# A Mamba-2 block with a quantised FFN on one core: high and low parts of the stationary tiles interleaved element by element, and shifted by 32, 64 and 96 bytes

## The reference, cut to what matters

```python
x = hidden_states                       # (2, 512, 512)
xn = layernorm(x)
# attention part (a Mamba-2 layer)
proj = xn @ in_proj_w.T                 # gate 8192, xBC 10240, dt 128 channels
gate, xBC, dt = split(proj)
xBC = silu(causal_conv4(xBC))           # per channel, 4 taps
xs, B, C = split(xBC)                   # 128 heads of 64; 8 groups of B and C, 128 wide
Y = ssd(xs, B, C, D, dt)                # chunks of 128 tokens
yg = Y * silu(gate)
out = yg * rsqrt(mean(yg**2 by group) + eps) * norm_w
s = out @ out_proj_w.T                  # 8192 -> 512
# FFN part, weights packed as 4-bit pairs with scales
h = silu(xn @ W1.T) * (xn @ W3.T)       # 512 -> 1376
g = silu(h @ W2.T)                      # 1376 -> 512
return x + s * g
```

## Time and profile before

| what | value |
|---|---|
| time, median of 3 runs | 1780.93 us (1780.87 to 1780.94) |
| the profiled execution | 1780.88 us, its span 1779.1 us |
| granted TensorE clock over the span | 0.999 of 2.4 GHz |
| TensorE matmul busy | 1764.8 us, 99% |
| VectorE, ScalarE, GpSimd busy | 80%, 69%, 71% |

### The profile page before, as it was taken

How to read it: one execution, slowest core, us unless ns; L and a number is a source line. 1 busy time by engine, 2 the same in 40 slices (tenths; PEclk the granted TensorE clock), 3 DMA queues, 4 the chain that set the end, 5 groups by cost and what they waited for, 6 DMA issues and landing times.

```text
span 1779.1 us, 30329 instructions
## 1 busy us (share of the span) xinstructions
PE 1764.8 (99%) x10357; PEld 1462.5 (82%) x10357; DVE 1427.7 (80%) x2196; ACT 1227.7 (69%) x2456; POOL 1261.9 (71%) x877
## 2 busy tenths in 40 slices
PE   8999999999999999999999999999999999999999
PEld 7788888888888888888888888888888888888877
DVE  7978878888788788788788887887887888878941
ACT  6986777777776777777867777677777677643320
POOL 5677787777777787677776787778776877676630
PEclk9999999999999999999999999999999999999999
DMA  5533343333333243333333333333333332235522
GB/s 197 165 124 101 100 131 108 94 122 107 117 107 111 97 134 96 101 111 119 117 105 98 117 124 96 116 101 115 122 90 112 109 127 96 78 109 166 150 77 95
DMA packets 122595, 202.84 MB, mean 114 GB/s; under 512 B 23056, under 2 KB 60560, under 8 KB 122192
## 3 DMA queue, kind: packets, MB, share of 16 engines
q1 hardware_dynamic: 120720, 197.32, 35.4%
q10 hardware_dynamic: 1728, 3.65, 0.5%
HBM read 193.57 MB, written 7.34 MB: 113 GB/s over the span
## 4 chain that ended last, share of the span: by engine, by line
PE 96%; DVE 2%; POOL 1%; issue 1%; DMA 0%; ACT 0%; SPq 0%; POOLq 0%; DVEq 0%
PE bank L135 17%; PE bank L137 17%; PE bank L136 16%; PE bank L544 11%; PE bank L586 7%; PE bank L632 6%; PE bank L634 6%; PE bank L633 6%; PE bank L832 3%; PE bank L694 3%; PE bank L675 1%; DVE z L1190 0%; PE bank L655 0%; DVE x_in L1342 0%; POOL yt L1523 0%
## 5 line engine op out<-in xcount | busy, mean ns | idle before, releaser
L1519 POOL TENSOR_TENSOR yt<-yt,ec 128x384 f32<-128x384 f32 x128 | 174.7, 1365 | 320.4 <-DVE ec L1254 320.4
L1190 DVE SCALAR_TENSOR_TENSOR z<-bank,cw_all,z 128x511 f32<-128x511 f32 (+2 forms) x477 | 356.2, 747 | 11.7 <-ACT z L945 0.4
L906 ACT ACTIVATE lm<-lm,hp 128x128 f32<-128x128 f32 x1024 | 313.2, 390 | 0.8
L135 PE MATMUL bank<-xn_hi,conv_hi 128*128 128x512 f32 x640 | 261.1, 408 | 3.5 <-DVE z L1190 3.5
L1224 DVE SCALAR_TENSOR_TENSOR lm<-lm,gm 128x1024 f32<-128x1024 f32 x128 | 261.0, 2039 | 3.5 <-ACT lm L906 3.5
L1245 DVE TENSOR_TENSOR xdt<-bank,hp 128x512 f32<-128x512 f32 x128 | 88.3, 690 | 212.8 <-PE bank L694 212.7
L137 PE MATMUL bank<-xn_hi,conv_lo 128*128 128x512 f32 x640 | 251.0, 392 | 0.0
L136 PE MATMUL bank<-xn_lo,conv_hi 128*128 128x512 f32 x640 | 250.7, 392 | 0.0
L1523 POOL TENSOR_TENSOR yt<-yt,gate 128x512 f32<-128x512 f32 x128 | 226.7, 1771 | 19.0 <-POOL yt L1519 0.9
L1528 POOL TENSOR_TENSOR conv_lo<-raw_x,conv_hi 128x512 fp32r<-128x512 f32 x124 | 218.9, 1766 | 9.8 <-ACT conv_hi L845 9.7
L135 PE MATMUL bank<-xn_hi,gate_hi 128*128 128x512 f32 x512 | 212.4, 415 | 0.0
(11 more groups left out here) (145 smaller groups left out, 3950.3 us busy)
## 6 DMA issues: line engine op xcount, KB each, us to landing
lm<-cs_d SPq DMA_DIRECT2D x128, 512.0 KB, 4.1
raw_x<-w_conv_dram SPq DMA_DIRECT2D x128, 256.0 KB, 3.1
ec<-e_d SPq DMA_DIRECT2D x256, 96.0 KB, 3.7
raw_o<-w_out_dram SPq DMA_DIRECT2D x64, 256.0 KB, 2.7
raw_g<-w_gate_dram SPq DMA_DIRECT2D x61, 256.0 KB, 2.8
raw_b<-w_conv_dram SPq DMA_DIRECT2D x32, 256.0 KB, 3.9
q_raw<-w1q_dram SPq DMA_DIRECT2D x10, 256.0 KB, 3.6
q_s<-w1s_dram SPq DMA_DIRECT2D x10, 256.0 KB, 3.9
```

Of the source, the lines that this page charges most:

```text
L135: pe.matmul(dst, a_hi, b_hi, start=(i == 0), stop=False)
L906: e = act.activation(lm[m % 3][:, u, :], lm[m % 3][:, u, :], ACT.Exp, bias=hp[bd.seq][:, Q_CS, k1, u:u + 1])
L1190: dve.scalar_tensor_tensor(dst[:, d:SEQ], src[:, 0:SEQ - d], cw_all[:, bd.group, pos, 3 - d:4 - d], dst[:, d:SEQ], ALU.mult, ALU.add).then ...
```

## The change

A new helper allocates a high and a low part together, as one tile whose last dimension is 2: element j of the high part is word 2j and that of the low part word 2j + 1. So a weight load still takes 128 words, each 8 bytes behind the one before, over 1024 bytes. ScalarE now writes each high part with a step of 8 bytes, and GpSimd reads it and writes the low part with that step. This holds for the stationary tiles of all five families. The moving tiles (`xn`, `wout`, `w2`) keep separate high and low parts.

Unnamed pads shift the tiles:

```diff
+        def alloc_pair(stack, name, shape):
+
+            t = alloc(stack, name, shape + [2], R32)
+            return t[:, :, :, 0], t[:, :, :, 1]
+
...
-        conv_hi = [alloc(main, f"conv_hi{i}", [KT, P], R32) for i in range(3)]
-        conv_lo = [alloc(main, f"conv_lo{i}", [KT, P], R32) for i in range(3)]
+        alloc(main, "off_c", [8])
+        conv_hi, conv_lo = zip(*[alloc_pair(main, f"conv_w{i}", [KT, P]) for i in range(3)])
...
-        gate_hi = [alloc(main, f"gate_hi{h}", [KT, HALF], R32) for h in range(2)]
-        gate_lo = [alloc(main, f"gate_lo{h}", [KT, HALF], R32) for h in range(2)]
+        alloc(main, "off_g", [8])
+        gate_hi, gate_lo = zip(*[alloc_pair(main, f"gate_w{h}", [KT, HALF]) for h in range(2)])
...
+        alloc(main, "off_o", [16])
         pre = ExitStack()
...
+        alloc(pre, "off_l", [24])
         wdt_lo = alloc(pre, "wdt_lo", [KT, P], R32)
+        alloc(pre, "past_y", [DIM])
...
-        y_hi = alloc(main, "y_hi", [2, SEQ], R32)
-        y_lo = alloc(main, "y_lo", [2, SEQ], R32)
+        alloc(main, "off_y", [24])
+        y_hi, y_lo = alloc_pair(main, "y_w", [2, SEQ])
...
-        up_hi = [[alloc(ctx, f"up_hi{i}{k}", [KT, P], R32) for k in range(2)] for i in range(2)]
-        up_lo = [[alloc(ctx, f"up_lo{i}{k}", [KT, P], R32) for k in range(2)] for i in range(2)]
+        up_hi, up_lo = zip(*[zip(*[alloc_pair(ctx, f"up_w{i}{k}", [KT, P]) for k in range(2)]) for i in range(2)])
...
-        h_hi = alloc(ctx, "h_hi", [MT + 1, SEQS * SEQ], R32)
-        h_lo = alloc(ctx, "h_lo", [MT + 1, SEQS * SEQ], R32)
+        h_hi, h_lo = alloc_pair(ctx, "h_w", [MT + 1, SEQS * SEQ])
```

## The result

The changed kernel takes **1803.36 us** (median of 4 runs, 1803.07 to 1804.4) against 1780.93: 22.4 us more, a ratio of 1.0127 with an interval of 1.0109 to 1.0144. The forecast of a modest gain has the wrong sign. The time lies in the range, among the slower cases. Lines in the changed file stand 6 further down from the allocations on.

What follows compares the result with a forecast made beforehand. TensorE's matmuls, busy 99% of the span, were taken to bound the kernel by their distances of starts. From 1780.9 us, less 8.3 for uneven and 5.8 for even stretches, 0 for the rest: 1766.8 us, range 1755 to 1806 (0.82).

Steps and rivals of the forecast that it cites:

- modest gain: Whole kernel: the likeliest case, 1755 to 1778 us around 1767, chance 0.45.
- the 96-column stretch: Four FFN groups with 96 weight columns: 230.0 ns a distance despite shorter loads, taken as best sign that TensorE's readers disturb each other.
- Fixed: TensorE's matmuls: changing weights costs what it costs; as the prediction's rival of no change, 1781 us, chance 0.18.
- The step of 8 bytes in the weight loads: Stationary tiles of all families: load and stream go at one pace, ending their disturbance; 8.3 us plus 5.8 us less.
- The 5.8 us for the even ones: 5751 evenly spaced matmuls in convolution, gate, output projection and FFN: each distance 1 ns shorter, 5.8 us less.
- The 8.3 us for the uneven stretches: 128 gate groups and 160 convolution groups: distances of 230.0 and 229.0 ns fall to 226.7, 8.3 us less.
- no change: Whole kernel: 13.3 ns is the cost of changing weights, unevenness comes from something else such as fp32 groups; 1781 us, chance 0.18.
- the left-over is the same at either width: TensorE's matmuls of 512 and 256 columns: 13.3 ns beyond streaming at both, ascribed to weight load or change of weights.
- The 1 ns from 388 against 389: One matmul without a load beside it took 388 ns, neighbours 389; the difference taken as gain for each even distance.
- The slower rival: Whole kernel: leaving equal steps and starts costs 3.3 ns a matmul, 1792 us, or twice 13.3 ns, 1849 us; chance 0.29.
- The fp32 matmuls: Plain fp32 matmuls between the families, operands now starting 32 bytes apart: 5 us either way, taken as 0.
- ScalarE and GpSimd: Their writes and reads with 8-byte steps: at most 1.5 us more a step on each, covered by waits, costed at nothing.

Runs made afterwards that it cites:

- e1: 24 series of 40 equal matmuls behind the last matmul of the kernel before, starts, steps and widths varied; step 4 at difference 0 took 226.7 ns, step 8 233.3.
- e7: Series of 36 equal matmuls behind the kernel before, both operands' starts varied; 226.7 ns with equal starts, 232.5 ns at 128 bytes apart.
- e11: Third set of series behind the kernel before: step 8 at further differences (231 to 234 ns), alternating starts, fewer moving columns (173.3 ns at 384, 216.7 at 480).
- e3: Changed kernel with high and low parts back in separate tiles, pads kept and added for the FFN tiles; 1807.77 us, 1.0150 against the kernel before.
- e2: Changed kernel without its pads: all five families interleaved, every tile at a multiple of 128 bytes; 1807.09 us, 1.0148 against the kernel before.

## Why the prediction was wrong

**What bounds the kernel** was read rightly. TensorE stayed at 99%, no idle time came or went, and the whole result is in distances of starts, with 21.5 of 22.4 us in distances of 512-column fp32r matmuls.

**That the two reads disturb each other, by how their positions run against each other**, was right too, and the 96-column stretch was the right sign: e1 has the same 230.0 ns with nothing else running. "Fixed" is refuted: e7 moves the distance between 226.7 and 233 ns by the starts alone. The Trainium skill ("SBUF — State Buffer", section "Who interferes with whom") has the two read ports of TensorE independent of each other; these runs do not agree, since the load's start alone moves the stream's distance by 6.6 ns.

**The step that failed** is "*The step of 8 bytes in the weight loads*", in its sentence "Where this distance is harmless, the disturbance is gone for the whole load". It took the 226.7 ns of the kernel before for a disturbed state that equal pace would relieve. It was the best that any series with 512 columns and two real operands reached: step 8 stands at 230.0 to 234 ns at all eight differences of 32 bytes, step 4 at 226.7 with equal starts and at 229 to 234 otherwise. Only with 32 weight columns, which the kernel doesn't have, did a step of 8 help (226.7 against 231.7). The 5.8 us for the even ones turned into a loss: 6.6 ns a matmul in the FFN, where I had −1.

**The 8.3 us for the uneven stretches** failed by a second error of the same step's working: they were taken for the same disturbance. The trace of before has them behind fp32 matmuls alone, 226.7 ns in the 30 convolution groups without such work ahead and 229.0 in the 124 with it. The rival "no change" named this cause. Nothing came back: the convolution went from 229.0 to 232.6 behind `state`. The gate is at 230.4 after 230.7, but by another way, since its distances no longer settle at 226.7 but keep to the 230 of a step of 8 at 64 bytes. That the two are equal is chance.

**That the left-over is the same at either width**, from 512 and 256 columns, was too general a reading: e11 has 13.3 ns at 384 and 16.7 at 480 and 496.

**The 1 ns from 388 against 389** The earlier trace rows was no measure of the disturbance. The length of one matmul without a load beside it says nothing on the distances. The series in which the stream reads one word was at 218.7 ns, so of the 13.3 ns over the bare streaming some 8 do depend on the addresses, while no shift or step with 128 weight columns and 512 moving ones brought any of them back.

**The slower rival** had the mechanism: equal steps and starts make 226.7 ns possible. Its price was too low. It took 230.0 from the uneven stretches for all families, 1792 us; the changed kernel's mean distance is 232.4, 4 ns above before and not 1.6. Its point of decision, 228.2, lies where the kernel before itself stands by the count of all traces (228.4). Its second branch, twice the 13.3 ns, did not occur. Its chance of 0.29 was too small beside 0.45 for a mechanism of which no row showed an instance; that leaving the pattern is dearer was in the 96-column row.

**The pads** as such cost time. I had them only as something that sets the distance; e3 shows that they cost about 22.8 us without any step, by its 27.0 less the 4.2 of its FFN tiles. The costs of pads and step don't add: 22.8 and 26.4 alone, 22.4 together. Against e2 the difference is in the gate, whose excess is 5.4 us at 64 bytes and 8.6 at 0.

**The fp32 matmuls** at 0: right. `c_t` with `state` is 277 ns before, in the changed kernel and in e3, with the starts apart or not. (By the count of 256 they are 160 bytes apart in the changed kernel.)

**ScalarE and GpSimd** at nothing: right. The copy took 49 ns more by its groups (617 before, 666 after) and the subtraction 16, some 0.2 us a step for 2.75 splits, against bounds of 1.5 us each and a slack of 2.5 us.

**The range** held the time because its upper part, up to 5.8 ns a matmul less 8.3 us, allowed for this rival. No row gave the 5.8; that the changed kernel's mean lies 5.7 ns above 226.7 is luck.

**What stays open** is what in the chip makes the pattern. With 128 weight columns and 512 moving ones it goes by the difference of starts modulo 256 bytes and the step, and it isn't the amount read by the load. Why fp32 work ahead makes the next ten distances uneven, and why 96 weight columns cost 3 ns more than 128, no run here settled.

## What to carry to other kernels

Where fp32r matmuls of 512 columns stand back to back with a new weight load each, give the stationary and the moving tile the same start modulo 256 bytes and read both with neighbouring words. Leaving this costs 2 to 8 ns a matmul, 0.9 to 1.5% of this kernel where all families left it, without any sign in waits or idle time; it shows only in the distance of starts. Other widths and fewer weight columns have to be measured by themselves. When two readings of such a small effect compete, a few dozen equal matmuls behind the kernel's last one give the number in one run. Before an unevenness is booked as something to win, look for groups of the same kind with something else ahead. And when a change leaves the one regular pattern that the trace shows to run best, ask first what the trace shows of places that leave it.

## What the runs showed of the hardware

- fp32r matmuls of 512 columns with a new load of 128 columns each: 226.7 ns from start to start with equal starts modulo 256 bytes and steps of 4 bytes, 228.8 to 234 ns at the other differences measured.
- Behind plain fp32 matmuls the distances of such a group are uneven for up to ten matmuls (229.0 and 230.7 ns on average), with tiles that stand at 226.7 behind other fp32r matmuls.
- Weight loads of 128 columns took 188 ns with steps of 4 bytes, 193 to 197 with 8, 253 with 12, 309 with 16, 331 with 32; the distance grew only to 245 ns, so a long load is mostly hidden.
- A moving tile read with a step of 8 bytes doubles the distance, to 451 ns.
- A load of one word repeated, and one of 32 columns, cost the stream as much (231.7 ns) as a shifted full one; a stream of one word runs at 218.7.
- ScalarE's write with a step of 8 bytes took 8% longer (666 against 617 ns), GpSimd's subtraction with it 1%.
